# A recurrent attention and expert kernel on one core: the second segment's U from halves of X and M in three fp32r passes, with Wq, Wk and M streamed through one pair of buffers

## What is computed

```python
xn = layernorm(x)
q, k, v = xn @ Wq + bq, xn @ Wk + bk, xn @ Wv + bv      # each (b, s, 4 heads, 256)
q, k = (q cos, q sin), (k cos, k sin)                    # phase rotation per head
attn = softmax(q . k / 16)                               # over the 4 heads g of one token, (b, s, h, g)
out = einsum('bshg,bsgd->bshd', attn, v)
s = swapaxes(out, 1, 2).reshape(b, s, 1024) @ Wo + bo
gates = sinkhorn((xn @ router_w.T + router_b) / temp)    # 8 experts, top 2
f = xn + sum over the top 2 of gate * ((relu(xn @ wg) * (xn @ wp)) @ wo)
result = x + s * silu(f)
```

## Time and profile before

| | us |
|---|---|
| runs | 1703.86 median of 3, 1700.03 to 1705.46 |
| the profiled execution | 1702.1 |
| its span | 1700.3 |
| TensorE busy | 1642.6 |
| VectorE busy | 985.6 |
| GpSimd busy | 785.9 |
| ScalarE busy | 734.0 |

### The profile page before, as it was taken

The page is one execution under the profiler, slowest core; times in us unless marked ns, Lnnn a source line. Parts: engine busy times, 40 slices in busy tenths (PEclk is TensorE's granted clock), DMA queues, the critical chain, the costliest instruction groups (busy, mean ns, idle before and its releaser), DMA issues.

```text
span 1700.3 us, 28610 instructions
## 1 busy us (share of the span) xinstructions
PE 1642.6 (97%) x9360; PEld 1276.4 (75%) x9360; DVE 985.6 (58%) x1879; ACT 734.0 (43%) x1205; POOL 785.9 (46%) x945
## 2 busy tenths in 40 slices
PE   5999899989999999999999999999999999999997
PEld 3456576678888888888888888776877668776785
DVE  7567889943333333333333335668777786777766
ACT  5774433413333333333333335356454564535542
POOL 4646497613433334343334432434634636345362
PEclk9999999999999999999999999999999999999999
DMA  9988833163313131313111412424555345552354
GB/s 331 397 318 282 286 113 125 45 238 127 129 52 125 57 125 56 124 55 125 54 56 57 152 54 87 162 100 155 180 186 198 125 150 178 192 182 94 127 168 137
DMA packets 162662, 250.96 MB, mean 148 GB/s; under 512 B 13928, under 2 KB 121248, under 8 KB 161376
## 3 DMA queue, kind: packets, MB, share of 16 engines
q1 hardware_dynamic: 147904, 211.47, 35.9%
q0 software_dynamic: 12960, 35.41, 6.2%
q10 hardware_dynamic: 1664, 2.26, 0.4%
HBM read 149.58 MB, written 99.50 MB: 146 GB/s over the span
## 4 chain that ended last, share of the span: by engine, by line
PE 83%; DMA 6%; DVE 4%; POOL 3%; SPq 2%; issue 1%; ACT 1%; ACTq 0%; DVEq 0%; POOLq 0%
PE ps L1135 20%; PE ps L1070 18%; PE ps L1017 12%; PE ps L1081 12%; PE ps L1154 10%; PE ps L1144 3%; DMA AUX<-xn_d,AUX 3%; PE ps L1038 2%; DMA AUX<-in_L_ffn_wo_dram 2%; PE ps L1117 2%; SPq L356 1%; PE ps L916 1%; POOL FR L609 1%; PE ps L972 1%; SPq L337 1%
## 5 line engine op out<-in xcount | busy, mean ns | idle before, releaser
L1135 PE MATMUL ps<-WR,FR 128*128 x1620 | 411.9, 404 | 5.2 <-issue 4.5
L1135 PEld LDWEIGHTS ps<-WR,FR 128*128 128x128 f32 x1620 | 298.7, 191 | 65.5 <-issue 7.3
L641 POOL DMA_INDIRECT y_d<-AUX x135 | 133.4, 988 | 369.7 <-ACT AUX L860 369.7
L1646 DVE TENSOR_TENSOR AUX<-AUX,ps 128x512 f32<-128x512 f32 x135 | 92.9, 688 | 350.3 <-ACT AUX L848 350.3
L809 ACT ACTIVATE WM<-ps,bcs,trig 128x512 f32<-128x512 f32 x256 | 255.9, 1019 | 90.7 <-PE ps L1070 83.1
L1586 DVE TENSOR_SCALAR WM<-ps,vec,trig 128x512 f32<-128x512 f32 x256 | 247.0, 996 | 63.3 <-ACT WM L809 62.5
L1017 PEld LDWEIGHTS ps<-WM 128*128 128x128 f32 x2048 | 232.3, 193 | 11.0 <-issue 6.2
L1017 PE MATMUL ps<-WM 128*128 128x128 f32 x2048 | 236.5, 277 | 3.5 <-DVE TM L1474 3.5
L1081 PE MATMUL ps<-WM,XTJ 128*128 128x512 f32 x512 | 237.8, 601 | 0.0
L848 ACT ACTIVATE AUX<-ps 128x512 f32<-128x512 f32 x135 | 80.9, 599 | 326.7 <-PE ps L1135 326.7
L1070 PE MATMUL ps<-XH,WH 128*128 128x512 f32 x512 | 204.7, 400 | 8.3 <-DVE WM L1586 6.4
(11 more groups left out here) (237 smaller groups left out, 2281.9 us busy)
## 6 DMA issues: line engine op xcount, KB each, us to landing
US<-u_d SPq DMA_DIRECT2D x63, 512.0 KB, 4.8
u_d<-UN SPq DMA_DIRECT2D x120, 256.0 KB, 2.0
WR<-w_d SPq DMA_DIRECT2D x8, 3072.0 KB
AUX<-y_d SPq DMA_DIRECT2D x32, 512.0 KB, 5.7
WM<-in_L_attn_x_dram SPq DMA_DIRECT2D x16, 512.0 KB, 9.8
xn_d<-WM SPq DMA_DIRECT2D x32, 256.0 KB, 7.1
AUX<-xn_d SPq DMA_DIRECT2D x16, 512.0 KB, 6.6
XB<-xn_d SPq DMA_DIRECT2D x30, 256.0 KB, 5.0
```

The lines of the kernel that those rows point to most:

```text
L641: e.indirect_dma_start(y_d, bass.IndirectOffsetOnAxis(toks[:, m - 5:m - 4], 0), YS[:, (m - 5) % 2, :], None).then_inc(s_y[(m - 5) % 2], 16)
L1135: mm = e.matmul(b[:, :], x, WR[:, bass.ds(off[m] + (2048 * z + 1024 * a + 512 * k), 512)], start=(k == 0 and x is xh and z == 0), stop=(k ...
L1646: e.tensor_tensor(HS[:, m % 2, :], GR[:, :], mP[m % 2][:, :], ALU.mult).then_inc(s_h, 1)
```

## The change

Only the second segment's arithmetic changes. M, already in DRAM from round 1, is split there during the expert tiles: `low(t)` on GpSimd, 48 steps at tiles 6 to 53, goes through 16 pieces of 512 columns in three steps each: load the piece (256 KB), copy it to a high half and subtract, store both halves. The high halves are loaded where M was (MH). The low halves stay in DRAM and are streamed in every round of the second segment into WH and WL, two blocks of U (2 x 512 KB) at a time: pair i as soon as block 4i+3 of Q and K is done. When two blocks of U are done, the pair is loaded again with its columns of the halves of Wq and Wk for the next round; these were stored to DRAM in round 1 (`wqk_d`, 8 x 512 KB, behind the store of M). A U block is then six fp32r matmuls: high X by high M, high X by low M, low X by high M. The stationary operand is read directly from the halves of X, every fourth token (`rearrange("p (r j) -> p j r", j=4)`). The halves of X have two sets of buffers by turns. GpSimd's XTJ adds fall away in the second segment, and the last round's x goes into XL's place.

```diff
...
         u_d = nc.dram_tensor("u_d", [N, H * D], F32).ap()
         y_d = nc.dram_tensor("y_d", [2 * N + NM * 128, D], F32).ap()
         m_d = nc.dram_tensor("m_d", [128, 8192], F32).ap()
+        mh_d = nc.dram_tensor("mh_d", [128, 8192], F32).ap()
+        ml_d = nc.dram_tensor("ml_d", [128, 8192], F32).ap()
+        wqk_d = nc.dram_tensor("wqk_d", [2, 4, 128, 1024], F32).ap()
         w_d = nc.dram_tensor("w_d", [E * 128, 6144], F32).ap()
         brow_d = nc.dram_tensor("brow_d", [32, 128], F32).ap()
 
...
         WM = sb("WM", [128, 24576])
         X = WM[:, 0:NT * D].rearrange("p (n d) -> p n d", d=D)
         M_s = WM[:, 16384:24576].rearrange("p (k n) -> p k n", k=2)
+        MH = WR[:, 16384:24576].rearrange("p (k n) -> p k n", k=2)
         with nc.sbuf_tensor("OH", [128, 8192], B16) as OH:
             pass
         with nc.sbuf_tensor("FR", [128, 8192], F32R) as FR:
...
 
         XB = sb("XB", [128, 4, D])
         XH = sb("XH", [128, 2, 512], F32R)
+        with nc.sbuf_tensor("XLF", [128, 4, D], F32) as XLF:
+            pass
         XL = sb("XL", [128, 2, 512], F32R)
+        with nc.sbuf_tensor("XTR", [128, 2, 512], F32R) as XTR:
+            pass
         XTJ = sb("XTJ", [128, 2, 4, 128])
+        with nc.sbuf_tensor("UNR", [128, 3, 512], F32R) as UNR:
+            pass
         UN = sb("UN", [128, 3, 512])
         US = sb("US", [128, 3, 4, D])
         TM = sb("TM", [128, 512])
...
         s_cl, s_ct, s_cg = (sem(n) for n in ("s_cl", "s_ct", "s_cg"))
         s_e1, s_et, s_eg, s_e2, s_eo, s_es = (sem(n) for n in ("s_e1", "s_et", "s_eg", "s_e2", "s_eo", "s_es"))
         s_wsp, s_md, s_xtj, s_gi = (sem(n) for n in ("s_wsp", "s_md", "s_xtj", "s_gi"))
+        s_wqk, s_mi, s_mo = (sem(n) for n in ("s_wqk", "s_mi", "s_mo"))
+        s_low = [sem(f"s_low{i}") for i in range(4)]
+        s_qkl = [sem(f"s_qkl{i}") for i in range(4)]
         s_ml = [sem(f"s_ml{j}") for j in range(4)]
         s_o = sem("s_o")
         s_sa2, s_pm, s_u63, s_c15, s_z, s_rl = (
...
         def cs(q):
             if q < NQ - 1:
                 return cY1, cY2, cN, cX
-            return cE1, cE2, cE3, AB[:, :, :].rearrange("p a (i d) -> p (a i) d", d=D)
+            return cE1, cE2, cE3, XLF[:, :, :]
 
         ends = cs(NQ - 1)
+
+        def xhl(q):
+
+            return (XTR, ABR) if q > QE and q % 2 else (XH, XL)
+
+        def pair(i):
+
+            return [w[:, :, 512 * i:512 * i + 512] for w in (WH, WL)]
 
         def us(n):
             return XB[:, :, :] if n == 4 * NQ - 1 else US[:, n % 3, :, :]
...
                 for h in range(H):
                     e.dma_start(rows(of, k)[h], cE3[h:128:4]).then_inc(s_es, 16)
 
+            def load_low(q, i):
+
+                e.wait_ge(s_ch, 24 * q + 4 * i + 4)
+                for z in range(2):
+                    a = 2 * i + z
+                    e.dma_start(pair(i)[z].bitcast(F32), ml_d[:, 1024 * a:1024 * a + 1024].rearrange("p (k n) -> p k n", k=2)
+                                ).then_inc(s_low[i], 16)
+
+            def load_qk(q, i):
+
+                e.wait_ge(s_ch, 24 * q + 16 + 2 * i + 2)
+                for z in range(2):
+                    e.dma_start(pair(i)[z].bitcast(F32), wqk_d[z, i].rearrange("p (k n) -> p k n", k=2)
+                                ).then_inc(s_qkl[i], 16)
+
             def segment(q0, q1):
                 for q in range(q0, q1):
                     if q + 1 < NQ:
...
                             store_half(i)
                     if q == 1:
                         e.dma_start(m_d, WM[:, 16384:24576]).then_inc(s_md, 16)
+                        e.wait_ge(s_wsp, 4)
+                        for i in range(4):
+                            for z in range(2):
+                                e.dma_start(wqk_d[z, i].rearrange("p (k n) -> p k n", k=2),
+                                            pair(i)[z].bitcast(F32)).then_inc(s_wqk, 16)
+                    if q >= QE:
+                        for i in range(4):
+                            load_low(q, i)
                     for c in range(8):
                         if q == 0:
                             continue
                         write_u(e, q, c)
+                        if QE <= q < NQ - 1 and c % 2:
+                            load_qk(q, c // 2)
                         if q > 0:
                             if c == 3:
                                 load_u(4 * q - 1)
...
                         load_c(q)
                     if q == NQ - 2:
                         e.wait_ge(s_es, 64 * QE)
+                        e.wait_ge(s_ch, 24 * (NQ - 1))
                         load_c(NQ - 1)
                 if q1 == NQ:
                     load_u(4 * NQ - 1)
...
                     e.wait_ge(s_u, x)
                 load_expert(x)
             spent(6)
+            e.wait_ge(s_wqk, 16 * 8)
+            e.wait_ge(s_mo, 32 * 16)
             for j in range(4):
                 cols = slice(1024 * j, 1024 * j + 1024)
-                e.dma_start(M_s[:, :, cols], m_d.rearrange("p (k n) -> p k n", k=2)[:, :, cols]).then_inc(s_ml[j], 16)
+                e.dma_start(MH[:, :, cols].bitcast(F32),
+                            mh_d.rearrange("p (k n) -> p k n", k=2)[:, :, cols]).then_inc(s_ml[j], 16)
             for i in range(2):
                 e.wait_ge(s_rs[i], 16 * 2 * (QE - 1))
                 e.wait_ge(s_y[i], 16 * ((NM - i + 1) // 2))
...
             e.wait_ge(s_gi, 1)
             for q in range(NQ):
                 e.wait_ge(s_x[q], 48)
+            def low(t):
+
+                p = t // 3
+                a, k = p // 2, p % 2
+                col = 4096 * k + 512 * a
+                raw, h, l = UN[:, 0, :], UNR[:, 1, :], UNR[:, 2, :]
+                if t % 3 == 0:
+                    if p == 0:
+                        e.wait_ge(s_md, 16)
+                        for i in range(3):
+                            e.wait_ge(s_uw[i], 16 * ((8 * QE - i + 2) // 3))
+                    else:
+                        e.wait_ge(s_mo, 32 * p)
+                    e.dma_start(raw, m_d[:, col:col + 512]).then_inc(s_mi, 16)
+                elif t % 3 == 1:
+                    e.wait_ge(s_mi, 16 * (p + 1))
+                    ch(e.tensor_copy(h, raw))
+                    ch(e.tensor_tensor(l, raw, h.bitcast(F32), ALU.subtract))
+                else:
+                    e.dma_start(mh_d[:, col:col + 512], h.bitcast(F32)).then_inc(s_mo, 16)
+                    e.dma_start(ml_d[:, 512 * p:512 * p + 512], l.bitcast(F32)).then_inc(s_mo, 16)
+
             for m in range(NM + 5):
+                if 6 <= m < 6 + 48:
+                    low(m - 6)
                 if m < NM:
                     if m >= 2:
                         e.wait_ge(s_gt, m - 1)
...
 
             e.wait_ge(s_gp, 2)
             for q in range(QE, NQ + 1):
-                if q < NQ:
-                    xtj(q)
                 if QE < q < NQ:
                     total(q - 1)
                 if q in host:
...
 
             def xt(q, k):
                 e.wait_ge(s_xt, 2 * q + k + 1)
-                if q:
+                if q > QE:
+                    e.wait_ge(s_ch, 24 * (q - 1))
+                elif q:
                     e.wait_ge(s_ch, 24 * q - 8)
                     e.wait_ge(s_xtj, 2 * q)
-                e.activation(XH[:, k, :], pXT[:, :], ACT.Copy).then_inc(s_xtc, 1)
+                e.activation(xhl(q)[0][:, k, :], pXT[:, :], ACT.Copy).then_inc(s_xtc, 1)
 
             xt(0, 0)
             e.wait_ge(s_wlo, 5)
...
                 for q in range(q0, q1):
                     e.wait_ge(s_xtc, 2 * q + 2)
                     e.wait_ge(s_xtd, 2 * q + 2)
+                    xh, xl = xhl(q)
                     for c in range(24):
                         b = ring(24 * q + c)
                         if c < 16:
+                            if q > QE and c % 4 == 0:
+                                e.wait_ge(s_qkl[c // 4], 32 * (q - QE))
                             for k in range(2):
-                                for w, xx in ((WH, XH), (WH, XL), (WL, XH)):
+                                for w, xx in ((WH, xh), (WH, xl), (WL, xh)):
                                     mm = e.matmul(b[:, :], w[:, k, 128 * c:128 * c + 128], xx[:, k, :],
-                                                  start=(k == 0 and w is WH and xx is XH), stop=(k == 1 and w is WL))
-                        else:
-                            if c == 16:
+                                                  start=(k == 0 and w is WH and xx is xh), stop=(k == 1 and w is WL))
+                        elif q < QE:
+                            a = c - 16
+                            if a == 0:
                                 e.wait_ge(s_xtj, 2 * q + 2)
-                                if q == QE:
-                                    e.wait_ge(s_ye, NM)
-                            a = c - 16
-                            if q == QE and a % 2 == 0:
-                                e.wait_ge(s_ml[a // 2], 16)
```

(14 more changed lines are left out.)

## The result

The change makes the kernel slower: 1763.14 us (1760.12 to 1767.17, 4 runs) against 1703.34 us (1700.03 to 1705.46, 4 runs), a ratio of 1.0351, 95% interval [1.0334, 1.0368]. The sign was forecast, the size was not: +59.8 us instead of +9.8, far outside the range. The profiled span went from 1700.3 to 1763.7 us, +63.4.

What follows compares the result with a forecast made beforehand. TensorE, busy 97% of the span, was taken as the bound. Second segment +2, round 1 +5.3 and expert tiles +2.5 gave +9.8 us on 1703.86: 1713.7 us; own range 1706 to 1720, whole range 1698 to 1728.

Steps and rivals of the forecast that it cites:

- (a): Rival: U ends with VectorE at 15.5 us because the u load lands 2.3 us sooner; -16 us, 1688 us, chance 0.12.
- (b): Rival: slowest DMA engine adds nothing (segment -6 us) and tiles hide the split; +0, 1703 us, chance 0.24.
- Rival (d): GpSimd becomes the bound of 48 expert tiles through slow DMA issues; +16 us over the forecast, 1730 us, chance 0.08.
- the landing of the load of u: In second-segment U: queued bytes delay this load to 16.0 us, so U ends at 17.8 us, 0.4 later than before.
- The rate: SP's queue in U: 4.72 MB ahead of and including the u load move at 388 GB/s, taking 12.2 us.
- The issue: SP in U: the u load's issue stays near 9.5 us into the stage; what grows is its flight.
- The upper bound: Second segment: +10 us at worst, with the engines' delay twice as large, against a forecast of +2 us.
- The strided weight load: U's matmuls: a stationary load at every fourth element takes 113 x 1.56 = 176 ns, under 227, so no loss.
- (c): Rival: strided weight load outlasts its covering matmul; at 300 ns +1.2 us in 12 rounds, 1726 us, chance 0.16.
- VectorE as the next bound of U: Second segment: 13.3 us of VectorE work keep U from ending before 15.5 us, so U gives at most 2.0 a round.
- Round 1: The Wq/Wk spill ahead of U stores delays the fourth mix from 225.91 to 231.2 us; cost 5.3 us.
- Tiles: Expert tiles: GpSimd's split steps delay gathers at three 3 MB expert loads, 0.8 us each; +2.5 us, 0 to +9.

Runs made afterwards that it cites:

- experiment 5: Changed kernel with the load of u behind the third U store, ahead of the reloads, and Wq/Wk's spill at round 2's start: 1697.5 us, ratio 0.9965 to before.
- experiment 10: Changed kernel with the spill in round 2 and the second Wq/Wk pair moved behind the load of u, still after the fourth U store: 1703.14 us.
- experiment 2: Changed kernel with each load of the streamed halves moving only 64 of 512 columns, same issues and waits: 1711.49 us (before 1703.37).
- experiment 7: As experiment 5, but U's stationary operand read from 128 contiguous columns instead of every fourth (tokens then wrong): 1688.46 us (before 1702.57).
- experiment 3: Changed kernel with the spill of Wq's and Wk's halves issued at the start of round 2 instead of round 1: 1752.79 us (before 1703.37).
- experiment 8: As experiment 5, without the 48 split steps; unsplit M loaded as both high and low halves: 1693.27 us, ratio 0.9931 to before.
- experiment 1: Changed kernel with the load of u moved behind the third U store, ahead of the Wq/Wk reloads: 1701.87 us, ratio 1.0000 to before.
- experiment 9: As experiment 5, but the first Wq/Wk pair stands ahead of the load of u again in rounds 4 to 14: 1699.12 us (before 1702.75).

## Why the prediction was wrong, step by step

**What held.** The place and the kind: the queue decides, a gap stands before the fourth mix (1 to 3 us forecast, 3.6 to 5.0 measured) behind the bias add that waits for the load of u; the line's content; the sign; round 1, where the load of u is issued at 225.75 (forecast 225.6). Rivals (a) and (b) would have needed the load in time. Rival (d) did not come: the stretch of the tiles is 7.4 us longer, 3.0 of them at a lower clock.

**The step that failed: the landing of the load of u**, put at 16.0 us into U and measured at 18.5. The split of these 2.5 us below is an estimate: the rate is measured in other windows than the landing, and the last term is what is left over.

- The rate. I took 4.72 MB at the 388 GB/s of a plain store: 12.2 us. Loads and stores mixed run at 340 GB/s when the share is 1.00 (round 9 of experiment 5), and 297 at 0.88 in U (338 for a full share, an estimate from the two): 14.0 us, +1.8. The Trainium skill (DMA: Bandwidth & Descriptors, Specifications) has some 358 GB/s for a core; I set it aside for the row of a store that was not of the kind in question. The rows now stand under the page's figure for mixed traffic and over it for the store. By that page's figure the landing would have been 17.0, an estimate, so the page alone would not have saved the forecast.
- The issue, which is no term of the sum by bytes, but says the same. It comes 10.4 us in, not 9.5: the second pair's two issues stand ahead of it, and the first mix and the strided U blocks are longer than I had them. In experiment 10, without that pair ahead, it is 9.0.
- The rest: 2.4 us are left (18.5 - 2.1 - 14.0) where I had 1.7 (0.6 + 0.3 + 0.8) for idle line and the slowest engine. Part of it is no idle line but more bytes. The window from the start of U to the landing in round 9:

```profile
1368.46:1386.97 18.51, 15.28 (x82) 12.87 (x80) 13.51 (x25) 8.39 (x12) 7.59 (x11) 1.00 0.86 283
```

283 GB/s over 18.51 us are 5.2 MB, 0.5 more than the 4.72 that I had counted as the line; the stores issued behind the load (the first 0.5 us later) were under way as well.

From the landing, the bias add and the mix were put at 1.8 us; they are 2.3, with a mix of 1.08 us at the lower clock. So U is 20.80 instead of 17.8, 3.0 us in each of eleven rounds.

**What was left out: the clock behind the gap.** I allowed for it in round 1 and not in the segment. TensorE has a granted clock of 1.00 in Q and K, 0.97 in U with its 3.60 us of idleness, and 0.93 in the scores, which take 15.50 us. Both are means of two levels: after idling from 1384.72 on, TensorE was granted 0.50 (1.2 GHz) from 1388.10 to 1391.50 and 1.00 again behind it:

```profile
1388.10:1391.50 3.40, 3.18 (x18) 2.40 (x19) 0.88 (x3) 1.58 (x2) 2.71 (x4) 0.50 1.04 372
```

The scores cost +1.3 us a round on the mean, +14 us. In experiments 2 and 5, whose gaps are 2.2 us and less, every score stage of rounds 4 to 14 has 1.00.

**The upper bound was not one.** +10 us doubled only the engines' delay and kept the rate at the one value that I had picked. With the rate at 338 and the issue at 10.4 in its working, the bound would have been near +36 us by my estimate, and the clock's 14 us would have taken it to about the +49 measured. The sum was near balance (the load "just landed"), so each us of error in the landing was multiplied by eleven rounds with nothing to absorb it.

**The strided weight load**, taken as free with rival (c) for more. It takes 309 ns, 1.64 times the 188 of a contiguous one; I had multiplied the right ratio (1.56, from GpSimd) with the wrong base, the 113 ns between two matmuls of the scores. A load's own duration stood in the trace of before and was not read (weight loads of U by line, ns min/median/max):

```profile
L1081 PEld LDWEIGHTS ps<-WM,XTJ x512: 186/190/337, 139.6 to 1670.3; 128*128 128x128 f32 x171
```

190 x 1.56 = 296 ns, over the 227 of the rival's condition. But (c)'s price was too high: loads overlap two matmuls in part, and the cost is 0.75 us a quiet round, some 6 us in all (experiment 7), not 1.2 on top of the queue's wait. In the change itself U waits for the load of u, and much of it is hidden. The Trainium skill (Advanced Engine Details and Errata, SBUF Cachelines) said that a line per element costs; these rows agree.

**VectorE** as the next bound of U, at 15.5 us: the number is near (15.57), the engine is not. The chain of a quiet round is TensorE without a gap, and with contiguous loads U goes to 14.82 us, under VectorE's floor as I had it. The 13.3 us of its work were no constant. The first masked add took 0.47 us in round 8 before (L1492), and takes in round 5 of experiment 7

```profile
1120.25 0.28 DVE L1582 TENSOR_TENSOR AC<-SA,mask 128x128 f32<-128x128 f32 x1
```

The difference goes with adds of GpSimd beside it, and not with XTJ, which falls away with the change. In round 8 before the adds of `total` (L660) ran there, and XTJ's (L571) in the scores:

```profile
1279.83 2.82 POOL L660 TENSOR_TENSOR AUX<-AUX 128x256 f32<-128x256 f32 x4
...
1298.83 4.51 POOL L571 TENSOR_TENSOR XTJ<-XH,XL 128x256 f32<-128x256 f32 x4
```

In round 5, where GpSimd adds nothing beside it, the add takes 0.28 us before the change too. VectorE binds in host rounds, at up to 1.75 us a bias add.

**Round 1**: 5.3 forecast, 6.7 measured (experiment 3). The issue was right; the mix comes at 232.57, 1.4 later than forecast, and its last wait is the landing of the store of s (231.9), which the sum had left out. **Tiles**: +2.5 forecast with 0 to +9; the waits for gathers grew by 3.7 and TensorE's idle time by 4.4, and experiment 8 puts the split's own part at about 1.6 to 3.5, inside the bounds. The rest of the stretch's 7.4 us is a lower granted clock (3.0), which differs as much between kernels with the same tiles; why it does stays open.

**Round 4** was to save 0.5, having no Silu: it took 20.98 like the others.

## What to carry to other kernels

When a change puts bytes ahead of a latency-bound load, draw up the line in front of that load and give its rate both ends from rows of the same kind of traffic; if the load is just in time now, multiply the miss by the rounds and take that as the upper bound. The mean share of the queues says little: the same bytes behind the load cost nothing at a share of 0.94. And read the duration of a weight load itself before calling a stride hidden.

## What the runs showed of the hardware

- A load of 128 columns of stationary fp32r operand from every fourth element takes 309 or 310 ns in the median, 187 or 188 contiguous; matmuls of 227 ns hide part of it (two U blocks of six matmuls each: 2.82 to 3.14 us strided, 2.72 to 2.96 contiguous; experiments 5 and 7).
- The granted clock: TensorE idle for 0.95 or 1.64 us kept its clock in the scores behind it (experiments 10 and 2); idle for 3.60 us it was granted 0.93 over the next 15.50 us (after); after gaps of 1.88 to 2.16 us it was 1.00 or 0.89 (1.00 in experiment 5, 0.89 in 1 and 9).
- Mixed loads and stores with the queues full: 340 GB/s (round 9 of experiment 5), against 388 in the window of the store of 4 MB.
- VectorE's add of 128x1024 takes 1.75 us instead of 1.21 when an add of GpSimd started some 0.1 us before it; when VectorE starts first, its own takes 1.21 and GpSimd's add of 128x256 1.79 instead of 0.73.
- An issue on SP's queue took up to 4.89 us with the store of M and the spill (8.4 MB) in line.
